# FFN 0's threshold search in rounds of three bits, and the X rows of FFN 0 and FFN 3 sent out during the attentions

## The reference

```python
x = x + tanh(g_xattn[i]) * xattn_i(layernorm(x), ctx_1024)
x = x + tanh(g_ffn[i]) * ffn_i(layernorm(x))
```

## Time and profile before

| | before |
|---|---|
| median of 3 runs | 2020.55 us (2018.66 to 2020.64) |
| profiled execution, time | 2014.52 us |
| profiled execution, span | 2012.6 us |
| TensorE granted clock, mean | 0.899 of full speed |
| busy: TensorE, its weight loads | 1630.8 us (81%), 1228.1 us (61%) |
| busy: VectorE, ScalarE, GpSimd | 1094.8 us (54%), 835.0 us (41%), 296.8 us (15%) |

### The profile page before, as it was taken

The page is one execution under the profiler, slowest core; times in us unless marked ns, Lnnn a source line. Parts: engine busy times, 40 slices in busy tenths (PEclk is TensorE's granted clock), DMA queues, the critical chain, the costliest instruction groups (busy, mean ns, idle before and its releaser), DMA issues.

```text
span 2012.6 us, 29431 instructions
## 1 busy us (share of the span) xinstructions
PE 1630.8 (81%) x10535; PEld 1228.1 (61%) x10536; DVE 1094.8 (54%) x2157; ACT 835.0 (41%) x1848; POOL 296.8 (15%) x351
## 2 busy tenths in 40 slices
PE   4999972595688874478887999999979863999997
PEld 3677760474455543335554678787745443999997
DVE  5555526513599998756663444535469956222221
ACT  3454430221777652335554622212289941222221
POOL 1101000441212000011110000000022101233332
PEclk8999975797789987679998999999989975999999
DMA  7535233124634224575524100000186534522221
GB/s 147 70 53 69 33 132 146 26 43 99 95 58 69 35 30 150 141 95 75 70 33 168 67 1 1 0 1 1 43 111 97 78 124 179 158 36 36 36 36 27
DMA packets 82713, 144.32 MB, mean 72 GB/s; under 512 B 13802, under 2 KB 68594, under 8 KB 79218
## 3 DMA queue, kind: packets, MB, share of 16 engines
q1 hardware_dynamic: 62626, 102.85, 22.1%
q0 software_dynamic: 19968, 39.87, 12.9%
HBM read 75.63 MB, written 27.79 MB: 51 GB/s over the span
## 4 chain that ended last, share of the span: by engine, by line
PE 59%; DVE 24%; ACT 5%; issue 5%; DMA 5%; SPq 2%; POOL 0%; DVEq 0%; POOLq 0%; ACTq 0%
PE ps L1253 12%; PE ps L1358 7%; PE ps L1369 7%; PE ps L893 4%; PE ps L1240 4%; DVE probs L1995 3%; PE ps L944 3%; DVE mx L1898 3%; PE ps L884 3%; PE ps L1173 2%; PE ps L1163 2%; PE ps L855 2%; ACT pT L1485 2%; PE ps L800 2%; DMA Qpack<-QP 2%
## 5 line engine op out<-in xcount | busy, mean ns | idle before, releaser
L1898 DVE TENSOR_REDUCE mx<-ps 128x2 f32<-128x512 f32 x256 | 169.7, 686 | 147.2 <-PE ps L858 76.2
L336 POOL DMA_DIRECT2D Kpack<-KP x192 | 101.5, 536 | 978.3 <-DVE KP L1860 854.7
L1480 ACT ACTIVATE pT<-ps 128x512 f32<-128x512 f32 x256 | 146.1, 595 | 165.1 <-PE ps L887 91.4
L884 PE MATMUL ps<-Qpack,Kpack 99*128 99x256 bf16 (+1 forms) x768 | 163.8, 283 | 29.8 <-ACT pT L1485 11.1
L855 PE MATMUL ps<-Kpack,Qpack 97*128 97x256 bf16 x512 | 118.3, 292 | 48.6 <-DVE mx L1898 27.6
L1358 PEld LDWEIGHTS ps<-xgT,XNT 128*128 128x128 f32 x1280 | 150.4, 193 | 2.0
L1358 PE MATMUL ps<-xgT,XNT 128*128 128x128 f32 x1280 | 150.5, 276 | 0.0
L1369 PE MATMUL ps<-w,mid 128*128 x640 | 144.6, 379 | 0.0
L1687 ACT ACTIVATE mid<-ps 128x512 f32<-128x512 f32 x80 | 43.4, 595 | 206.8 <-PE ps L1358 201.9
L884 PEld LDWEIGHTS ps<-Qpack,Kpack 99*128 99x128 bf16 (+1 forms) x768 | 67.9, 100 | 98.7 <-ACT pT L1485 37.5
L1369 PEld LDWEIGHTS ps<-w,mid 128*128 128x128 f32 x640 | 118.6, 190 | 14.5
(11 more groups left out here) (302 smaller groups left out, 3306.7 us busy)
## 6 DMA issues: line engine op xcount, KB each, us to landing
Kpack<-KP POOLq DMA_DIRECT2D x192, 128.0 KB, 5.3
Qpack<-QP SPq DMA_DIRECT2D x192, 128.0 KB, 7.0
w<-in_w SPq DMA_DIRECT2D x16, 1024.0 KB, 6.7
ctxT<-in_ctxT SPq DMA_DIRECT2D x32, 256.0 KB, 7.6
h<-h_rows SPq DMA_DIRECT2D x2, 4096.0 KB, 22.2
wd<-in_wd SPq DMA_DIRECT2D x4, 1536.0 KB, 14.7
xn_rows<-xn SPq DMA_DIRECT2D x16, 256.0 KB, 3.6
wu<-in_wu SPq DMA_DIRECT2D x4, 768.0 KB, 11.6
```

What stands on the lines that cost most here:

```text
L336: eng.dma_start(Kpack[j][DH * k:DH * (k + 1)].rearrange("d (e f) t -> d e (f t)", f=HALF), KP[par][:, part]).then_inc(done, 16)
L884: mm = pe.matmul(A[h % ring][:, t], Kpack[par][0:rows, h, t * P:(t + 1) * P], Qpack[par][0:rows, h], start=True, stop=L != 0)
L1480: act.activation(pT[h % 8][:], A[h % 2][:], ACT.Exp).then_inc(s["exp_done"], 1)
L1898: dve.tensor_reduce(mx[:, :, h], A[2 + h % 2][:], AX.X, ALU.max).then_inc(s["smax_done"], 1)
```

## The change

It has two parts.

1. **The search** takes three bits a round, in ten rounds, two of them unrolled. A round has 7 candidates, so `above` is 7 x 16 x 8 elements. TensorE counts them in four matmuls of 7 x 4 x 8 = 224 columns, one for each group of four tiles, which add up in one PSUM bank; VectorE then sums 4 values for each of 56 sums.
2. **The X rows** of FFN 0 and FFN 3 are no longer sent together when the stage begins. `send_rows(n, b)` sends one batch, 256 KB, with batch 0 also the two spare tiles, and waits for that batch's residual. It stands at the end of SP's slots of attentions 0 and 3, for batch b-1 (attention 0) or b-2 (attention 3). Batch 7 (FFN 0), or 6 and 7 (FFN 3), are left for the stage itself. In FFN 3 `send_normed` now stands ahead of expert 0's load. POOL waits for 10 DMAs of a table where it waited for 6.

```diff
--- before.py
+++ after.py
@@ -48,7 +48,8 @@
 TOP0 = T // E0
 SL0 = TOP0 // P
 
-DIGIT_BITS, DIGITS, UNROLL0 = 2, 15, 3
+DIGIT_BITS, DIGITS, UNROLL0 = 3, 10, 2
+COUNTED0 = 4
 DIGIT = (1 << DIGIT_BITS) - 1
 HID = 1024
 HT = HID // P
@@ -423,8 +424,18 @@
             def load_ctx(b, par):
                 sp.dma_start(ctxT[par][:], a["ctxT"][:, :, ds(b * S, S)]).then_inc(ctx_sem[par], 16)
 
+            def send_rows(n, b):
+
+                rows = table[stages[n][1]]
+                sp.wait_ge(s["x_res"], FREE + 8 * order["att", stages[n][1]] + b + 1)
+                sp.dma_start(rows[b * S:(b + 1) * S].rearrange("(t p) c -> p t c", p=P), X[:, ST * b:ST * b + ST]).then_inc(s["rows_ready"], 16)
+                if b == 0:
+                    sp.dma_start(rows[T:T + P], X[:, 0]).then_inc(s["rows_ready"], 16)
+                    sp.dma_start(xn_rows[T:T + P], X[:, 0]).then_inc(s["rows_ready"], 16)
+
             def attention(n, L):
                 i = order["att", L]
+                sends, lag = ("ffn", L) in GATHERED, 1 if L in SOFTMAX_KEYS else 2
                 if n > 0:
                     ready_x(sp, n)
                 load_ctx(0, 0)
@@ -486,6 +497,8 @@
                         load_ctx(b + CTX_RING, b % CTX_RING)
                     if L in SOFTMAX_KEYS and exists(b + 1):
                         max_rows(b + 1)
+                    if sends and exists(b - lag):
+                        send_rows(n + 1, b - lag)
 
                 def packs1(b):
                     j = b % 2
@@ -514,16 +527,6 @@
                         max_rows(0)
                     slots_keys(slot_keys)
 
-            def send_rows(n):
-
-                rows = table[stages[n][1]]
-                for part in range(4):
-                    tiles = slice(part * NT // 4, (part + 1) * NT // 4)
-                    sp.dma_start(rows[0:T].rearrange("(t p) c -> p t c", p=P)[:, tiles], X[:, tiles]).then_inc(s["rows_ready"], 16)
-
-                sp.dma_start(rows[T:T + P], X[:, 0]).then_inc(s["rows_ready"], 16)
-                sp.dma_start(xn_rows[T:T + P], X[:, 0]).then_inc(s["rows_ready"], 16)
-
             def send_normed(n):
                 normed = xn_rows[0:T].rearrange("(t p) c -> p t c", p=P)
                 with sp.Fori(0, PAIRS // LNB) as t:
@@ -537,7 +540,7 @@
                     sp.dma_start(wr0[:], a["wr0"]).then_inc(s["f0_router"], 16)
                     sp.dma_start(br0[:], a["br0"].partition_broadcast(P)).then_inc(s["f0_router"], 16)
                     sp.dma_start(bu0[:], a["bu0"]).then_inc(s["f0_router"], 16)
-                    send_rows(n)
+                    send_rows(n, B - 1)
                     send_normed(n)
                     for g in range(NG0):
                         sp.dma_start(wu0[:, g], a["wu0"][:, g]).then_inc(s[f"experts_w{g}"], 16)
@@ -559,14 +562,15 @@
                     sp.dma_start(s3_2[:], a["s3_2"].partition_broadcast(P)).then_inc(s["f2_w3"], 16)
                 else:
                     sp.dma_start(wr3[:], a["wr3"]).then_inc(s["f3_router"], 16)
-                    send_rows(n)
+                    for b in range(B - 2, B):
+                        send_rows(n, b)
 
                     def load(e):
                         sp.dma_start(w1_3[:, e], a["w1_3"][e]).then_inc(s[f"experts_w{e}"], 16)
                         sp.dma_start(w2_3[:, e], a["w2_3"][e]).then_inc(s[f"experts_w{e}"], 16)
 
+                    send_normed(n)
                     load(0)
-                    send_normed(n)
                     for e in range(E3):
                         if e == E3 - 3:
 
@@ -665,7 +669,7 @@
 
             def rows_sent(n):
 
-                pool.wait_ge(s["rows_ready"], 6 * 16 * (g_order[stages[n]] + 1))
+                pool.wait_ge(s["rows_ready"], (B + 2) * 16 * (g_order[stages[n]] + 1))
                 for j in range(LNB):
                     pool.wait_ge(xn_out[j], SENT0 + 16 * (PAIRS // LNB) * (g_order[stages[n]] + 1))
 
@@ -1131,8 +1135,10 @@
                 with pe.Fori(0, DIGITS // UNROLL0) as i:
                     for d in range(UNROLL0):
                         pe.wait_ge(s["thr_cmp"], UNROLL0 * i + d + 1)
-                        pe.matmul(ps[1][:].rearrange("p a b -> p (a b)")[:, 0:DIGIT * NT * E0], ones_bf[:],
-                                  above[:].rearrange("p j t e -> p (j t e)"), start=True, stop=True).then_inc(s["thr_cnt"], 1)
+                        for t in range(0, NT, COUNTED0):
+                            mm = pe.matmul(ps[1][:].rearrange("p a b -> p (a b)")[:, 0:DIGIT * COUNTED0 * E0], ones_bf[:],
+                                           above[:, :, t:t + COUNTED0], start=t == 0, stop=t + COUNTED0 == NT)
+                        mm.then_inc(s["thr_cnt"], 1)
 
                 pe.wait_ge(s["thr_cmp"], DIGITS + 1)
                 counts(0, ps[2], 2 * NT * E0)
@@ -2168,7 +2174,7 @@
                         dve.tensor_tensor(above[:], probs_e[:].unsqueeze(1).to_broadcast(wide),
                                           cand[:].bitcast(F32).unsqueeze(2).to_broadcast(wide), ALU.is_ge).then_inc(s["thr_cmp"], 1)
                         dve.wait_ge(s["thr_cnt"], UNROLL0 * i + d + 1)
-                        counted = ps[1][:].rearrange("p a b -> p (a b)")[:, 0:DIGIT * NT * E0]
+                        counted = ps[1][:].rearrange("p a b -> p (a b)")[:, 0:DIGIT * COUNTED0 * E0]
                         chain(k + 2, dve.tensor_reduce(cnt[:], counted.rearrange("p (j t e) -> p j e t", j=DIGIT, e=E0), AX.X, ALU.add))
                         chain(k + 3, dve.scalar_tensor_tensor(reached[:], cnt[:], TOP0 - 0.5, step_f[:], ALU.is_ge, ALU.mult))
                         dve.tensor_scalar(step_f[:], step_f[:], 0.5 ** DIGIT_BITS, None, ALU.mult)
```

## The result

The changed kernel takes **2004.86 us** in the median of 5 runs (1999.16 to 2007.46), the kernel before, run beside it, 2020.64 (2018.66 to 2024.16). The ratio is 0.992, with a 95% interval of 0.9908 to 0.9932: 13.7 to 18.6 us faster. Forecast were 2006.1 us and a range of 2000.5 to 2011.5. The profiled execution took 2003.19 us, its span 2001.3.

What follows compares the result with a forecast made beforehand. It took FFN 3's and FFN 0's routers to wait on normed pairs' landings and the search to be a VectorE-TensorE ping-pong; -4.5 - 1.3 - 8.7 + 0 = -14.5 us from 2020.55 gave 2006.1 us, range 2000.5 to 2011.5.

Steps and rivals of the forecast that it cites:

- the three terms: Search -4.5 us, FFN 0's router -1.3 and FFN 3's router -8.7, summing to -14.5 us.
- The search, -4.5: Threshold search: ten rounds of 3.68 us for fifteen of 2.76, -4.6 us, with 0.1 given back by memsets.
- The matmul term: Search round: four counting matmuls of 224 columns take 0.93 us, +0.43, each further one costing its columns only.
- the rival with dear matmuls: Search: each of the four matmuls pays its own start-up, so the search gains nothing, 2011.4 us; chance 7%.
- the small operations: Search round on VectorE: `cand`, `reached`, `taken` +0.03 us each, `step_f` and `step_i` +0.03 together; sum +0.13.
- FFN 3's router, -8.7: FFN 3 before the logits: TensorE's turns follow at 2.45 us without the gap, 1650.90 against 1659.58, -8.7 us.
- FFN 0's router, -1.3: FFN 0 before the logits: TensorE's turns follow at 2.45 us without the gap, 292.52 against 293.83, -1.3 us.
- the first rival: Routers: with the gap closed TensorE's granted clock rises, -3.3 us in each stage, 1999.5 us; chance 5%.
- if PEclk leaves 0.5 before the logits: Routers: a stated sign of being wrong, TensorE's granted clock moving off 0.5 before the router's logits are ready.
- The wait: VectorE's wait for an `xn` buffer in both routers shrinks to 1 or 2 us, from 5.15 and 12.36.
- The sends, 0: Attentions 0 and 3: the X sends moved there cost 0, from bounds 0 and 11.4 us.
- The offset: Whole kernel: the profiled execution was 6 us faster than the median 2020.55, and that difference carries over.

Runs made afterwards that it cites:

- the two halves: Two runs on the kernel before: the three-bit search alone, 2015.84 us, and the moved X rows alone, 2006.03 us.
- two_bits_grouped: The kernel before, still 15 rounds of two bits, with only its counting matmul split into four over groups of tiles: 2015.3 us, ratio 0.9978.
- changed_again: The changed kernel unaltered, run a second time on the chip of other follow-up runs: 1999.62 us, ratio 0.9903.
- rows_behind: The changed kernel with no sends in the attentions, all eight batches of X sent in their own stage behind the normed pairs: 2003.3 us, ratio 0.9921.
- expert_ahead: The changed kernel with FFN 3's expert 0 asked for ahead of the normed pairs again: 2006.67 us, ratio 0.9935.
- sends_three: The changed kernel with every send of a batch of X made three times, the extra two into DRAM nobody reads: 2004.59 us, ratio 0.9924.
- search_only: The kernel before with the three-bit search alone, X rows sent in the stages as before: 2015.84 us, ratio 0.9982.
- kept_busy: The changed kernel with 20 unread 512-column matmuls on TensorE ahead of the first transposes of FFN 0 and FFN 3: 1992.17 us, ratio 0.9874.

## Why the prediction held, point by point

- **Time and sum.** 14.5 us forecast, 16.2 by the ratio (13.7 to 18.6). The stages at 1.2 GHz give 4.1 + 1.3 + 8.4 = 13.8, so the three terms are right as a sum; that the two halves' medians also make 14.5 to the decimal is luck, with some 4 us of uncertainty on it, and so is part of how near 2004.86 is to 2006.1.
- **The search, -4.5: measured -4.1.** The round was 3.73 us for 3.68. The matmul term, the one without a row of its own, came out at 0.93, and the rival with dear matmuls is refuted; `above` and `cnt` were exact too. The 0.05 lies in the small operations, `cand`, `reached` and `taken` at 0.22 to 0.24 each, and ten times it is about the 0.4 that is missing. What the forecast had wrong was the reading: it laid the smallness of the gain on the wider rounds, which is true of the third bit (3.73/3 = 1.24 us a bit, 2.46/2 = 1.23 with two bits grouped), but did not see that the grouping alone gives all of it.
- **FFN 3's router, -8.7: measured -8.4.** The beat of 2.45 us and the idle time that goes were right, and the gain reaches the end: from the square root to the end of the span FFN 3 took 372.3 us before and 363.2 after. In FFN 0 the same holds to about 1 us (flags to attention 1's square root 140.5 before, 141.0 after, 140.2 to 141.6 elsewhere).
- **FFN 0's router, -1.3: exact at 1.2 GHz, 24.4 to 23.1, and 6.2 us too small in the profiled execution.** The step that failed is the first rival's "transposes and 8-column products did nothing in those 13 us, and nothing in their kind changes. 5%", with its sum that lets the clock rise only past 13 us. It rose at about 286.3, TensorE having worked without a break since 282.93, in two of seven profiles, and in two_bits_grouped even with the gap left open. By its own sign of being wrong, "if PEclk leaves 0.5 before the logits", the prediction was wrong here. The stretch of the earlier trace rows was one execution in which it had not risen, and I took it for a property of the work. With what the later profiles show, a chance of two in seven for FFN 0 and a prize of 6 us there would have been the reading. How often it rises in unprofiled runs is not measured; changed_again's median, 1999.62, lies 5 us below 2019.13 - 14.5, which would fit, and does not show it. What makes it rise in one execution and not in another stays open. The Trainium skill says ("TensorE: Matmul & The Clock Gate", Part 1) that sustained activity opens the gate, and (Part 4) that for transposes the full clock does not engage. changed_again stands against the first as enough by itself, with TensorE busy for 4.00 of 4.00 us and 0.50 from 284 to 292. The windows of 286 to 292 stand against the second as a rule for this mix of transposes and small products: 1.00 with nothing else in TensorE's queue.
- **The wait.** "1 or 2 us" was 0.76 in FFN 0 and, above the bound, 2.46 in three pieces in FFN 3. That the amount ahead of the pairs makes the rest of the 12.36 is shown by rows_behind and expert_ahead; 2.48 us stay with no row of X ahead, and those are the landing itself. They cost nothing, since TensorE has pairs in hand.
- **The sends, 0.** Right, and sends_three shows it with three times the traffic, to the few us by which the attentions differ between executions (266.7 to 268.8 and 190.8 to 194.9 in the table). The expert behind the normed pairs gives no sign of a cost: FFN 3 from its exponential to the first gather took 34.5 us for 35.0, and 33.7 to 35.0 over all kernels.
- **The offset.** The profile before was called 6 us fast and the difference carried over, which was right. Against search_only and two_bits_grouped, which leave the attentions alone as well, it was short in attention 2 (250.9 for 254.1 and 254.0) and attention 3 (191.8 for 193.5 and 194.2), about 5 of the 6 us. Such differences are why the spans differ by 11.3 us where the runs differ by 15.8.

## What to carry to other kernels

In this kernel a buffer that comes back by a DMA was late by what had been asked for ahead of it, and cost only what went beyond the work that its consumer still had in hand: put that traffic behind the pieces in the same queue, and moving it to another stage may be needless. Where a loop alternates between two engines, look first at who does the adding and at what can start on half the data, and then at the number of rounds. When a wait in front of TensorE goes, price what follows at both clocks, since a stretch that is newly without gaps may get the other one.

## What was not expected of the hardware

- In FFN 0's router TensorE's granted clock went from 0.50 to 1.00 on transposes and 8-column products alone in two of seven profiles, and in two_bits_grouped, and stayed at 0.50 for the same work in the other five. A turn is 1.28 us at the one and 2.45 at the other.
- It also falls under load: in kept_busy's FFN 0 from 1.00 to 0.50 within 288 to 292, PE busy 4.00 of 4.00 us there; in the changed kernel between 292 and 294.
- Accumulating matmuls of 96 bf16 columns were as cheap by the column as one of 384: 0.50 us both ways at the granted clock 0.50, with four weight loads in 0.29 us beside them.
- The same attention code differs by 3 to 4 us between executions (292.9 to 296.1, 250.9 to 255.1) with the mean granted clock 0.01 to 0.02 apart, a fifth to a quarter of what the whole change is worth.
